# Two layers over a graph: the second edges of two steps share one buffer and one maximum, and seven rows are fetched where six were

## The reference

```
h = max(layernorm(x), 0)
x = x + M(h)                  # M: for every node, feature by feature, the maximum of h over its neighbours
h = max(layernorm(x), 0)
x = x + elu(softmax(e) @ (h W))   # e[i,j] = leaky_relu(hW a1[i] + hW a2[j]) where adj[i,j] > 0, else -9e15
```

## Time and profile before

| what | value |
|---|---|
| median of 3 runs | 742.16 us (742.04 to 742.75) |
| span of the profiled execution | 753.0 us |
| granted TensorE clock, mean | 0.990 |
| PE busy | 681.6 us (91%) |
| DVE busy | 693.7 us (92%) |
| ACT busy | 473.1 us (63%) |
| POOL busy | 281.8 us (37%) |
| steps of the first layer | from 27.4 to some 481 us |
| share of DMA engines' time in 160 to 240 us | 0.85 |

### The profile page before, as it was taken

One profiled execution on the slowest core, in us unless ns is written; L12 is line 12 of the kernel. 1 busy time (PEld: TensorE's weight loads), 2 busy tenths in 40 slices (PEclk: granted clock), 3 DMA queues, 4 the chain that ended last, 5 costly groups with the idle time before them and its releaser, 6 DMA issues.

```text
span 753.0 us, 14749 instructions
## 1 busy us (share of the span) xinstructions
PE 681.6 (91%) x5560; PEld 490.6 (65%) x5560; DVE 693.7 (92%) x1023; ACT 473.1 (63%) x685; POOL 281.8 (37%) x259
## 2 busy tenths in 40 slices
PE   1788999999999999999999998699999999999994
PEld 1344655555555555555555554498998999999994
DVE  8999999999999999999999999988998999889893
ACT  3888999889898899998999897562433111001000
POOL 0612034434434535444444355441620294134040
PEclk9999999999999999999999999799999999999998
DMA  9999978997888888888888746342531544443400
GB/s 305 310 355 390 344 230 270 303 327 239 268 249 247 273 258 237 272 265 241 261 263 265 246 143 228 103 143 71 187 130 62 219 140 158 156 177 130 165 15 17
DMA packets 63000, 163.07 MB, mean 217 GB/s; under 512 B 6416, under 2 KB 11152, under 8 KB 58832
## 3 DMA queue, kind: packets, MB, share of 16 engines
q1 hardware_dynamic: 53776, 138.75, 54.2%
q0 software_dynamic: 9152, 23.34, 12.1%
HBM read 117.51 MB, written 44.56 MB: 215 GB/s over the span
## 4 chain that ended last, share of the span: by engine, by line
PE 53%; DVE 31%; issue 12%; ACT 2%; DMA 1%; DVEq 0%; another core or an unknown queue 0%; SPq 0%
PE pick_ps L714 23%; DVE acc L867 20%; PE pick_ps L613 17%; DVE rest L1054 5%; PE late_ps L627 4%; PE late_ps L585 4%; PE order_ps L594 2%; PE late_ps L693 1%; PE late_ps L623 1%; DMA best<-x 1%; DVE left L889 1%; ACT depth L403 1%; DVE found L915 1%; PE late_ps L714 1%; PE order_ps L680 1%
## 5 line engine op out<-in xcount | busy, mean ns | idle before, releaser
L867 DVE TENSOR_TENSOR acc<-pick_ps,acc 128x1024 f32<-128x1024 f32 x248 | 302.6, 1220 | 20.9 <-PE pick_ps L613 12.6
L363 POOL DMA_INDIRECT found<-subset_max,tops x192 | 204.4, 1065 | 271.8 <-DVE acc L867 187.5
L1054 DVE SCALAR_TENSOR_TENSOR rest<-depth,curves_sb,stage 128x512 f32<-128x512 f32 x256 | 199.5, 821 | 15.3 <-PE pick_ps L714 3.1
L714 PE MATMUL pick_ps<-keys,rest 128*128 128x129 f32 x1792 | 207.7, 276 | 3.3 <-DVE rest L1054 3.2
L714 PEld LDWEIGHTS pick_ps<-keys,rest 128*128 128x128 f32 x1792 | 204.6, 193 | 7.4 <-DVE rest L1054 5.8
L402 ACT ACTIVATE first<-order_ps 128x1024 f16<-128x1024 f32 x128 | 131.9, 1030 | 39.1 <-PE order_ps L594 33.0
L403 ACT ACTIVATE depth<-order_ps 128x1024 f16<-128x1024 f32 x128 | 131.5, 1027 | 0.0
L613 PE MATMUL pick_ps<-first,h_hi 128*128 128x512 f16 x256 | 97.3, 380 | 17.6 <-DVE acc L867 17.1
L613 PE MATMUL pick_ps<-second,h_hi 128*128 128x512 f16 x256 | 97.2, 380 | 15.2 <-DVE acc L867 14.7
L585 PEld LDWEIGHTS late_ps<-ident_h,stage 128*128 128x128 f16 x1024 | 68.4, 99 | 50.0 <-DMA stage<-adj 12.9
L613 PE MATMUL pick_ps<-first,h_lo 128*128 128x512 f16 x256 | 97.4, 380 | 0.0
(11 more groups left out here) (146 smaller groups left out, 599.9 us busy)
## 6 DMA issues: line engine op xcount, KB each, us to landing
stage<-adj SPq DMA_DIRECT2D x64, 1024.0 KB
edge_units<-edge_t SPq DMA_DIRECT2D x64, 512.0 KB
stage<-edge_units SPq DMA_DIRECT2D x32, 1024.0 KB, 4.8
subset_max<-keys POOLq DMA_DIRECT2D x13, 512.0 KB, 9.0
found<-subset_max,tops POOLq DMA_INDIRECT x192
best<-x SPq DMA_DIRECT2D x4, 512.0 KB, 5.9
subset_max<-x POOLq DMA_DIRECT2D x4, 512.0 KB, 6.6
out<-keys POOLq DMA_DIRECT2D x7, 256.0 KB, 2.8
```

The costliest lines, as they stand in the source:

```text
L363: nc.gpsimd.indirect_dma_start(found[:, n % NG, s, :], None, subset_max, bass.IndirectOffsetOnAxis(tops[:, n, s:s + 1], 0)).then_inc(gathe ...
L714: last = nc.tensor.matmul(out_ps(q, b), weight[:, n % WEIGHTS, b * P:(b + 1) * P], wh[:, c, :], start=c == 0 and starts(q, b), stop=c == C ...
L867: V.tensor_tensor(acc[:, q % 2, :], pick_ps[k][:, :], acc[:, q % 2, :], ALU.max).then_inc(raised, 1)
L1054: V.scalar_tensor_tensor(out=weight[:, n % WEIGHTS, :], in0=limit[:, q % 4, :], scalar=slope[:, c:c + 1], in1=units[:, m % EDGES, k * TI:( ...
```

## The change

What the steps compute is arranged anew for every pair of an even and an odd step:

- In the odd step's rank, two further products with a constant weight of 0.25 (carry_w) add the even step's second one-hot, so that an odd step's second edge counts as second only where the even step has none in the same column of the pair; otherwise it goes to the rest. That rank therefore waits for the even step's seconds.
- The second edges of both steps are picked with eight products into one buffer (pick_joint), and one take reads it. There are 192 takes where there were 256. The three picks of a pair of steps alternate between the two buffers.
- ACT makes the odd step's first with a sigmoid instead of a relu, and the even step's depth ahead of its first. Its rests (later) are gone: DVE makes all of them, and the 512-wide product L623 of every other digest is gone too.
- seconds are made for one step at a time, 1024 wide, at other places of DVE's order; the first one stands in the start-up.
- Seven rows are fetched for a block, the eighth key shows an overflow. The gathers wait for takes counted anew. halve_two stays at its steps; its second instruction is twice as wide.

The core of the diff:

```
-FETCHES = 6
+FETCHES = 7
...
+        def pick_of(g):
+            return 3 * (g // 2) + g % 2
+        def joint_of(m):
+            return 3 * m + 2
...
-                            pool.wait_ge(raised, 2 * (STEPS + 2 + QUAD * n) + 4 + s)
+                            pool.wait_ge(raised, pick_of(STEPS + 2 + QUAD * n) + 3 + s)
...
-                    nc.scalar.activation(first[:, g % 4, :], order_ps[:, :], ACT.Relu, scale=-1.0, bias=1.0 - MARK).then_inc(first_ready, 1)
+                    if g % 2:
+                        nc.scalar.activation(first[:, g % 4, :], order_ps[:, :], ACT.Sigmoid, scale=-SHARP, bias=SHARP * (1.0 - 1.5 * CARRY - MARK)).then_inc(first_ready, 1)
                     nc.scalar.activation(depth[:, g % 4, :], order_ps[:, :], ACT.Abs, bias=MARK - MID).then_inc(depth_ready, 1)
+                    if g % 2 == 0:
+                        nc.scalar.activation(first[:, g % 4, :], order_ps[:, :], ACT.Relu, scale=-1.0, bias=1.0 - MARK).then_inc(first_ready, 1)
...
                         pe.wait_ge(depth_ready, g)
+                        pe.wait_ge(first_ready, g)
                     for c in range(PAIR):
                         last = nc.tensor.matmul(order_ps[:, c * TI:(c + 1) * TI], order_w[:, :], edge_t[:, g % (KEPT * KEEP), c * TI:(c + 1) * TI],
-                                                start=True, stop=True)
+                                                start=True, stop=g % 2 == 0)
+                    if g % 2:
+                        pe.wait_ge(second_ready, g)
+                        for c in range(PAIR):
+                            last = nc.tensor.matmul(order_ps[:, c * TI:(c + 1) * TI], carry_w[:, :], second[:, (g - 1) % 4, c * TI:(c + 1) * TI],
+                                                    start=False, stop=True)
...
+                def pick(n, parts):
+                    if n >= 2:
+                        pe.wait_ge(raised, n - 1)
...
+                def pick_joint(m):
+                    pe.wait_ge(second_ready, 2 * m + 2)
+                    pick(joint_of(m), [(g % STEPS, second[:, g % 4, :]) for g in (2 * m, 2 * m + 1)])
...
-                        V.tensor_tensor(found[:, at, 0:3, :], found[:, at, 0:3, :], found[:, at, 3:6, :], ALU.max).then_inc(halved, 1)
+                                dve.wait_ge(gathered[b % NG][k], 16 * fetched(k) * (b // NG + 1))
+                        V.tensor_tensor(found[:, at, 0:3, :], found[:, at, 0:3, :], found[:, at, 4:7, :], ALU.max).then_inc(halved, 1)
...
-                        V.tensor_tensor(found[:, at, 0, :], found[:, at, 0, :], found[:, at, 1, :], ALU.max).then_inc(halved, 1)
+                        V.tensor_tensor(found[:, at, 0:2, :], found[:, at, 0:2, :], found[:, at, 2:4, :], ALU.max).then_inc(halved, 1)
...
+                seconds(1)
                 for g in range(PAIRS):
+                    if g % 2 == 0 and g + 2 < PAIRS:
+                        seconds(g + 2)
+                    take(pick_of(g))
+                    if g % 2 == 0:
                         rests(g // 2)
+                    elif g + 2 < PAIRS:
+                        seconds(g + 2)
...
+                    if g % 2:
+                        take(joint_of(g // 2))
```

More of the change, by code:

```diff
@@ L611, in pick @@
                     for c in range(PAIR):
-                        for part, half_h in enumerate((h_hi, h_lo)):
-                            last = nc.tensor.matmul(pick_ps[k][:, c * TI:(c + 1) * TI], half_h[:, p * PAIR + c, :],
-                                                    s[:, c * TI:(c + 1) * TI], start=part == 0, stop=part == 1)
+                        for i, (p, one_hot) in enumerate(parts):
+                            for part, half_h in enumerate((h_hi, h_lo)):
+                                last = nc.tensor.matmul(pick_ps[n % 2][:, c * TI:(c + 1) * TI], half_h[:, p * PAIR + c, :],
+                                                        one_hot[:, c * TI:(c + 1) * TI], start=i + part == 0, stop=i == len(parts) - 1 and part == 1)
@@ L615, in pick, with pick_first @@
                     last.then_inc(picked, 1)
+                def pick_first(g):
+                    pe.wait_ge(first_ready, g + 1)
+                    if g < STEPS // 4:
+                        pe.wait_ge(lo_first, 1)
+                    elif g < STEPS:
+                        pe.wait_ge(lo_ready, g * PAIR // EIGHTH - 1)
+                    pick(pick_of(g), ((g % STEPS, first[:, g % 4, :]),))
+                def pick_joint(m):
+                    pe.wait_ge(second_ready, 2 * m + 2)
+                    pick(joint_of(m), [(g % STEPS, second[:, g % 4, :]) for g in (2 * m, 2 * m + 1)])
@@ L627, in digest @@
                             last = nc.tensor.matmul(key_ps[:, r * P:(r + 1) * P], rest[:, g % RESTS, c * TI + r * P:c * TI + (r + 1) * P],
[L628 removed]
+                                                    bit_w[:, b, :], start=r == 0 and b == 0, stop=r == ROWS - 1 and b == QUAD - 1)
                     last.then_inc(digested, 1)
@@ L726, in _ @@
                 for g in range(PAIRS):
-                    pick(g, 0)
+                    pick_first(g)
                     if g + 3 < PAIRS:
@@ L739, in _ @@
                         rows(1)
-                    pick(g, 1)
+                    if g % 2:
+                        pick_joint(g // 2)
                     if g + AHEAD < PAIRS:
@@ L852, in rests @@
                 def rests(m):
                     at, to = 2 * m % 4, 2 * m % RESTS
+                    dve.wait_ge(depth_ready, 2 * m + 2)
                     if 2 * m >= RESTS:
                         dve.wait_ge(digested, 2 * (m - RESTS // 2 + 1))
-                    V.tensor_scalar(rest[:, to:to + 2, :], depth[:, at:at + 2, :], MID - 1.5, float(GROUPS), ALU.is_lt, ALU.add).then_inc(rest_even, 1)
-                def take(g, k):
-                    q, p = g // STEPS, g % STEPS
-                    dve.wait_ge(picked, 2 * g + k + 1)
-                    if p == 0 and k == 0:
+                    V.tensor_scalar(rest[:, to:to + 2, :], depth[:, at:at + 2, :], MID - 1 - CARRY / 2, float(GROUPS), ALU.is_lt, ALU.add).then_inc(rest_ready, 1)
@@ L933, in x_scale @@
                         if k == 3:
+                            seconds(0)
                             dve.wait_ge(hi_ready, 1)
@@ L1020, in _ @@
                         moments(1)
-                    take(g, 1)
+                    if g % 2:
+                        take(joint_of(g // 2))
                     if g < len(CHAINS):
                         chain(g)
-                    if p == 0 and q >= 1:
-                        fold(q - 1)
+                    if p == 0 and g:
+                        fold(g // STEPS - 1)
                     n, i = (g - STEPS - 2) // QUAD, (g - STEPS - 2) % QUAD
```

103 lines of the change are left out of this document (36 added, 67 removed).

## The result

The changed kernel takes 775.01 us (median of 4 runs, 772.06 to 778.8) against 742.45 for the kernel before (4 runs): the ratio is 1.0437, with a 95% interval of 1.0404 to 1.0470. It is 32.6 us slower; 50 were forecast, and a time of 792. The time lies in the stated range and the direction is the one forecast, by a sum in which two terms were off, in opposite directions.

The account below looks back on a forecast made before the run. DVE was taken to set the steps' pace, PE having some 10% to spare. Terms 7.5 + 36 + 3.4 + 3.5 made 50 us, so 742.2 + 50 = 792 us; range 757 to 822.

Parts of the forecast that it names:

- all but the gathers: Forecast terms besides the seventh gather: 7.5 us over the 100 steps from 24 on, 3.4 for steps 12 to 23, 3.5 earlier.
- Part 1: Steps: less work on DVE, 5.75 us a pair, more on PE, 6.53; PE alone would be 0.37 a pair better.
- Part 2: Hand-over of order_ps: PE waits 0.52 us for ACT before each even rank; a pair takes 7.05, 7.5 us over 100 steps.
- Part 3: Seventh gather, let go just before halve_two: DVE waits at 13 halvings, 2.77 us each, 36 us, ends 5 and 67.
- L - 2.83: Cost in us of each halve_two, L being a gather's time to land: 5.6 taken, ends 3.2 and 8.0.
- the last arrivals: Last rows' later arrival in the second layer: priced at nothing, 1 to 3 us if the cover fails.
- Part 4: First 24 steps: +3.4 us for steps 12 to 23, +2.3 for the twelve before, +1.2 in the start-up.
- Only the hand-over: Rival: a gather lands within 2.8 us, so only the wait for order_ps counts: 757 us, chance 0.17.
- The clock: Rival: waits at the 13 halvings also lower PE's clock, 1.7 us each, 22 us more: 814 us, chance 0.12.
- Faster: Rival: hand-over hidden and gathers in time, PE's 6.53 a pair sets the pace: 723 us, chance 0.09.

Follow-up runs that it names:

- the last two runs: Changed kernel with split joint picks, earlier gathers, seconds ahead and halvings behind rests, 736.21 us; then the same with whole joint picks, 761.56 us.
- the best version: Changed kernel with split joint picks, earlier gathers, seconds directly behind the joint take, and halvings behind rests in even steps without a search: 736.21 us, ratio 0.9915.
- halvings out of the way: Changed kernel with whole joint picks, earlier gathers, seconds directly behind the joint take, and halvings behind rests in even steps without a search: 761.56 us.
- gathers earlier: Changed kernel with the sixth and seventh gather of a block let go by the same take as the fifth: 768.14 us.
- second profile of before: Kernel before, unchanged, profiled once more because the first profile's span was 753.0 us: measured 743.06 us, span 740.8.

## Why the prediction was right, and where not

Taken in this order, the last two runs cut the 32.6 us into three parts: from before to the best version -6.2 (what less work on DVE and more on PE is worth with all of it in good places, 736.21); the hand-over of order_ps +25.3 (761.56); and what stands around the gathers and halvings +13.4 (775.01). The parts depend on the order: taken out first, in the changed kernel, the hand-over was worth 12.4. Against the sum of the prediction, all but the gathers was forecast at 14 and cost 19.1, and the gathers were forecast at 36 and cost 13.4. The two errors hide a part of each other: with the gathers' alone, the forecast would have lain 22 us off instead of 17. To that extent its closeness is luck. The range held because both ends for the gather were kept.

**Part 1** was right. PE needs 6.53 a pair as worked out. DVE is at 65.08 / 80 x 7.15 = 5.82 a pair, against 5.75; a 1024-wide seconds takes 433 ns, against 420.

**Part 2** had the mechanism and the pair, 7.05 against 7.01 measured, and the wait, 0.52 against 0.48. What failed was what it was compared with: 6.90 from a long execution instead of 6.72. So the term was 0.15 a pair and should have been 0.29; over 100 steps 14.5 us instead of 7.5.

**Part 3 was the step that failed**, by its size. The geometry was right (DVE at the halving 2.09 us behind the gather's start, against 2.0), DVE did wait 13 times, and the formula of L - 2.83 a halving holds where a gather was late. In DVE's and PE's timelines (a halving, and the even ranks around it) and the landing of the gather at 161.54, which it waited for:

```profile
166.30 0.96 DVE L886 TENSOR_TENSOR found<-found 128x768 f32<-128x768 f32 x1 [2.67 <-DMA found<-subset_max,tops]
...
164.70 0.59 PE L590 MATMUL order_ps<-edge_t,order_w 128*128 128x512 f16 x2 [0.32 <-issue]
173.53 0.59 PE L590 MATMUL order_ps<-edge_t,order_w 128*128 128x512 f16 x2 [0.32 <-issue]
...
DMA to landing us min/median/max: 4.6/4.6/4.6
```

From 4.6 the formula makes 1.8; the pair takes 8.83, 1.82 over 7.01. But L was taken as 5.6, the middle. In the twelve halvings ahead of the last, DVE's waits sum to 21.3 - 6.0 = 15.3 us, 1.28 each; behind 2.09, and less the 0.2 from landing to halving, that makes L 3.2 on average, the low end of the earlier trace rows. By the prediction's own formula 0.4 a halving follows from 3.2, not 2.77. With halvings out of the way the 80 steps take 280.5, in the changed kernel 286.1: 5.6 us for 10 halvings, 0.56 each.

I had argued from the DMA share of 0.85; that is a mean, and a gather meets what the DMA engines do at its moment. Windows of 2.8 us from the start of a gather: the one at 248.51 (landed after 2.8), the one at 244.95 with gathers earlier (5.7), and one with six gathers in the changed kernel (5.9). The share of the DMA engines is the last number but one; it counts a transfer where it starts, so it can pass 1:

```profile
248.51:251.31 2.80, 2.80 (x26) 1.58 (x23) 1.90 (x3) 1.72 (x3) 2.19 (x3) 1.00 0.43 116
...
244.95:247.75 2.80, 2.80 (x26) 1.75 (x25) 1.76 (x3) 2.34 (x4) 1.03 (x1) 1.00 1.06 406
...
243.93:246.73 2.80, 2.80 (x27) 1.77 (x25) 1.76 (x4) 2.20 (x4) 0.95 (x1) 1.00 1.05 409
```

The seventh gather of the changed kernel starts where the engines run empty between two loads of stage, which SP issues at 243.07 and 250.08. Its distance from the sixth, 2.39 us, isn't the reason: the one with six gathers comes 2.86 behind its predecessor and lands after 5.9, as POOL's timeline and its landing show:

```profile
241.07 1.15 POOL L370 DMA_INDIRECT found<-subset_max,tops  x1 [0.81 <-DVE acc L870]
243.93 0.95 POOL L370 DMA_INDIRECT found<-subset_max,tops  x1 [1.71 <-DVE acc L870]
...
DMA to landing us min/median/max: 5.9/5.9/5.9
```

This is read from three gathers; no run moved the loads of stage by themselves. The page "DMA: Bandwidth & Descriptors" of the Trainium skill, section "Anatomy of one DMA — SWDGE (gpsimd) path", would let this term vanish, by an estimate of 2.15 us: nearer to the outcome than my choice, though no gather with a recorded landing was that fast, and the median of 5.4 is more than twice it.

The prediction priced the last arrivals at nothing, "1 to 3 us" without cover. This was too little: 12.7 us lie behind step 112, of which eight pairs at the difference of the steps are 3.4; among the rest are the 6.04 at the last halving, when the second layer's loads of edge_units had begun, and 2.85 at the last block. With gathers earlier 9.3 of the 12.7 are gone.

**Part 4** had its sum about right, and two of its terms wrong: 6.9 were forecast up to step 24, and 5.4 are found. In DVE's timelines, first of the second profile of before, where the second of the two takes in a row begins steps 12 and 24, then of the changed kernel:

```profile
74.48 2.53 DVE L867 TENSOR_TENSOR acc<-pick_ps,acc 128x1024 f32<-128x1024 f32 x2
112.76 2.55 DVE L867 TENSOR_TENSOR acc<-pick_ps,acc 128x1024 f32<-128x1024 f32 x2
...
77.40 1.23 DVE L870 TENSOR_TENSOR acc<-pick_ps,acc 128x1024 f32<-128x1024 f32 x1 [0.20 <-PE pick_ps L605]
119.48 1.22 DVE L870 TENSOR_TENSOR acc<-pick_ps,acc 128x1024 f32<-128x1024 f32 x1 [0.20 <-PE pick_ps L605]
```

A take lasts 1.22, so steps 12 and 24 begin at 75.79 and 114.09 before, at 77.40 and 119.48 now; the first take stands at 27.64 and 29.66. The start-up thus costs 2.0 (forecast 1.2), steps 0 to 11 -0.4 (forecast 2.3), steps 12 to 23 3.8 (forecast 3.4). The 2.3 rests on a misreading of the earlier trace rows: 74.19 is the second take of step 11, so 46.8 us are eleven and a half steps, and twelve took 48.1. The mechanism is there, the chain ahead of the seconds; but before, these steps were as slow. DVE's timeline now, first takes of two pairs following each other:

```profile
60.07 1.22 DVE L870 TENSOR_TENSOR acc<-pick_ps,acc 128x1024 f32<-128x1024 f32 x1 [0.76 <-PE pick_ps L605]
61.22 1.22 DVE L846 TENSOR_TENSOR keys<-keys,x 128x1024 f32<-128x1024 f32 x1
62.35 0.42 DVE L852 TENSOR_SCALAR second<-depth 128x1024 f16<-128x1024 f16 x1
...
67.86 1.23 DVE L870 TENSOR_TENSOR acc<-pick_ps,acc 128x1024 f32<-128x1024 f32 x1 [0.76 <-PE pick_ps L605]
```

A pair takes 7.79; with the seconds ahead of the chains and whole picks it is 6.93 (56.93 to 63.86), 0.86 less, where 0.85 was worked out.

**Rivals.** *Only the hand-over* (757) underrated the term of Part 2, and comes near what is measured with halvings out of the way, 761.6. *The clock* did not fall at the halvings within the steps: the window of 160 to 240 has 1.00, that of 130 to 470 too, with PE waiting 0.5 us at every even rank. Behind the last halving it did, in PE's timeline and the window from 484 to 490 (clock 0.72):

```profile
486.10 0.58 PE L605 MATMUL pick_ps<-first,h_hi 128*128 128x512 f16 x1 [3.53 <-DVE acc L870]
...
484.00:490.00 6.00, 3.83 (x16) 1.82 (x16) 5.93 (x11) 0.51 (x1) 2.11 (x2) 0.72 0.80 283
```

Idle gaps in a loop that throw the clock back, as the Trainium skill's page "TensorE: Matmul & The Clock Gate", section "HAM oscillation — how this bites in real kernels", describes them, don't show at gaps of 0.5 us; behind the waits of 3.53 us here and 2.73 us at 586.78 the clock did fall. Over the whole execution the mean granted clock is 0.986, against 0.989 in the second profile of before. *Faster* is the last version but one: with hand-over and halvings hidden PE sets the pace at 6.53, as that rival had it, though with 736 and not 723, since its 723 also started from 6.90.

## What to carry to other kernels

When work is moved from one engine to another at a tie, look at what stands between two hand-overs of a shared buffer: here 0.48 us a pair undid the gain, and moving four products behind another instruction brought pairs without a halving back to PE's own 6.53. An idle time that is taken away can be worth little until what stands behind it on the same engine is no longer late: the halving's wait, the seconds behind it and the take behind it came to the fore in turn, and only a place with room for the work ended this. And take a pace from a profile only after comparing its span with the median of the runs.

## What I had not expected of the hardware

The time in which an indirect gather of 64 KB lands ranges from 2.8 to 8.5 us within one execution. In the gathers looked at it goes with the share of the DMA engines in the first 2.8 us (0.43: 2.8; 1.05 and 1.06: 5.9 and 5.7), and not with the distance from the gather before (2.8 at 2.39 us, 5.9 at 2.86, 5.7 at 1.26). Starting one 3.6 us sooner (244.95 against 248.51) made it land 0.7 sooner, in a kernel that is itself some 1 us ahead there. Seven gathers instead of six cost the kernel before 13.4 us, though DVE came to the halving 6.8 us behind the start of the last one.
